# Delta attention of the last layer in chunks of 32 tokens, all batches in lockstep, one quarter of the partitions per head

## The reference, cut to what matters

```python
q, k = l2norm(q), l2norm(k); v = v * beta; kb = k * beta      # beta = sigmoid(x @ Wb), per token and head
# per chunk of 32 tokens: T = inverse of (I + strictly lower part of kb @ k^T)
u, w = T @ v, T @ kb
def step(S, (qi, ki, ui, wi)):                                 # over the chunks, in order
    attn = where(i >= j, qi @ ki^T, 0)
    u_i = ui - wi @ S
    o_i = qi @ S + attn @ u_i
    return S + ki^T @ u_i, o_i
```

## Time and profile before

| | us |
|---|---|
| runs of the kernel before, median of 3 | 8943.74 |
| lowest and highest run | 8923.92, 8946.13 |
| the profiled execution, its own time | 8934.45 |
| its span, first to last instruction | 8932.6 |
| sublayer 6 up to its router, in that span (7437.3 to 8450.4) | 1013.1 |

### The profile page before, as it was taken

One profiled execution on the slowest core, in us unless ns is written; L12 is line 12 of the kernel. 1 busy time (PEld: TensorE's weight loads), 2 busy tenths in 40 slices (PEclk: granted clock), 3 DMA queues, 4 the chain that ended last, 5 costly groups with the idle time before them and its releaser, 6 DMA issues. The chain is left out here.

```text
span 8932.6 us, 296414 instructions
## 1 busy us (share of the span) xinstructions
PE 7426.1 (83%) x129614; PEld 5361.2 (60%) x129614; DVE 5916.2 (66%) x11095; ACT 4144.6 (46%) x6987; POOL 2904.6 (33%) x2116
## 2 busy tenths in 40 slices
PE   7998799999996987987987997997986784756666
PEld 3443588888885665665665665665664453645634
DVE  6664477777776876876866866866866667244266
ACT  3554244444444765765765765765752122111121
POOL 0110122222223753754754745745730000100000
PEclk9998699999998999999999999999998896555556
DMA  0000000000001221221212212212210000000000
GB/s 14 1 1 1 5 5 5 5 5 5 5 3 50 72 59 47 73 54 52 73 50 57 70 47 61 69 44 66 69 40 0 14 0 2 3 2 2 4 0 12
DMA packets 190372, 256.44 MB, mean 29 GB/s; under 512 B 58253, under 2 KB 84748, under 8 KB 188172
## 3 DMA queue, kind: packets, MB, share of 16 engines
q1 hardware_dynamic: 189068, 237.31, 10.0%
HBM read 27.45 MB, written 2.10 MB: 3 GB/s over the span
## 5 line engine op out<-in xcount | busy, mean ns | idle before, releaser
L1758 PE MATMUL wa_front<-w_wqkv,wa_xsT 128*128 128x512 f32 x2400 | 1197.7, 622 | 53.2 <-PEq L66 24.4
L1680 POOL TENSOR_TENSOR XNT<-XNT 128x1024 f32<-128x1024 f32 x396 | 938.2, 2369 | 257.3 <-DVE XNT L1864 257.3
L1683 POOL TENSOR_TENSOR XNT<-XNT,wa_rnorm 128x1024 f32<-128x1024 f32 x396 | 754.2, 1904 | 438.1 <-DVE wa_rnorm L1872 438.1
L1861 DVE TENSOR_TENSOR XNT<-wa_front,w_scaled 128x1024 f32<-128x1024 f32 x396 | 472.4, 1193 | 381.2 <-ACT wa_sq L1699 279.8
L1758 PEld LDWEIGHTS wa_front<-w_wqkv,wa_xsT 128*128 128x128 f32 x2400 | 416.8, 194 | 387.5 <-issue 364.8
L1699 ACT ACTIVATE wa_sq<-wa_front 128x1024 f32<-128x1024 f32 x402 | 408.5, 1016 | 222.6 <-PE wa_front L1758 222.6
L1864 DVE TENSOR_TENSOR XNT<-wa_front,w_scaled 128x512 f32<-128x512 f32 x792 | 505.7, 680 | 0.0
L1877 DVE TENSOR_REDUCE wa_norm<-wa_sq 128x16 f32<-128x1024 f32 x396 | 478.7, 1209 | 0.0
L446 PE MATMUL a0h_ring<-a0h_QT,a0h_KT 32*128 32x512 f32 (+3 forms) x1536 | 449.0, 556 | 14.3 <-ACT a0h_E L564 10.4
L564 ACT ACTIVATE a0h_E<-a0h_ring 128x512 f32<-128x512 f32 (+1 forms) x640 | 320.6, 554 | 287.9 <-PE a0h_ring L446 285.8
L1764 PEld LDWEIGHTS wa_front<-consts,XNT 128*128 128x128 f32 x3168 | 358.7, 142 | 150.6 <-issue 74.5
(11 more groups left out here) (582 smaller groups left out, 18296.2 us busy)
## 6 DMA issues: line engine op xcount, KB each, us to landing
wa_v_look<-wa_v_all SPq DMA_DIRECT2D x1188, 128.0 KB, 2.3
wa_v_look<-wa_v_all SPq DMA_DIRECT2D x792, 64.0 KB, 2.0
w_wqkv<-in_L_ffn_Wqkv_dram SPq DMA_DIRECT2D x6, 1024.0 KB
w_wo<-in_L_ffn_Wo_dram SPq DMA_DIRECT2D x6, 512.0 KB
w_wqkv<-in_L_ffn_Wqkv_dram SPq DMA_DIRECT2D x12, 256.0 KB
f2w_raw<-in_L_ffn_w_dram SPq DMA_DIRECT2D x48, 64.0 KB, 1.9
out_dram<-X SPq DMA_DIRECT2D x1, 2048.0 KB, 8.7
w_w<-in_L_ffn_W_dram SPq DMA_DIRECT2D x6, 341.0 KB
```

Of the source, the lines that this page charges most:

```text
L1680: g.tensor_tensor(rot[:, at], rot[:, at], part[:, at], ALU.add).then_inc(s[summed], 1)
L1683: g.tensor_tensor(rot[:, at], rot[:, at], spread(rnorm[:, at, :], HDW), ALU.mult).then_inc(s[done], 1)
L1758: last = pe.matmul(front[:, first + i, :], xsT[:, slot, :], wqkv[:, (2 * n + i) * 512:(2 * n + i + 1) * 512], start=True, stop=True)
L1861: v.tensor_tensor(rot[:, n], src, cos, ALU.mult)
```

## The change

The chunks become 32 tokens long, as in the reference, and the batches are no longer worked in pairs: there are four paths stages and then a single chunk stage, in which a step covers 4 chunks x 4 batches = 16 matrices for each head. Head h lives on partitions quarter(h), in SBUF and in the array, through all products. Levels 5 and 6 are gone, and with them Nc, T64, Zt6. Keys are not normalized: their norm goes into the factor bp = beta/(k.k) of the rows, and v is multiplied by the norm. The product with w is made once a step (WT), and the recurrence runs over the 4 chunks of a step one after the other (`look`, `weigh`, `learn`, `remember`), between the levels of the inverse. In the paths stage the keys and v are turned head by head, in 32x32 blocks (`turn_heads`, 128 matmuls each), and the small sums come as 8 + 128 + 128 matmuls in place of 24; the mid convolution goes to `act[:, 2, :]`. The products still go through the same three engines, and no DMA changes.

The diff, cut to its core (declarations, copies of constants and index arithmetic left out):

```diff
+CHUNK3 = 32
+CHUNKS3 = SEQ // CHUNK3
+PER = P // CHUNK3
...
 # l3_paths_steps, PE
+            def turn_heads(out, src, sem):
+                for n in range(CHUNKS3):
+                    at = slice(n * CHUNK3, (n + 1) * CHUNK3)
+                    for h in range(HEADS3):
+                        last = pe.matmul(out[quarter(h), at], src[quarter(h), at], c.ident[quarter(h), quarter(h)], start=True,
+                                         stop=True)
+                last.then_inc(sem, 1)
...
-            turn(rawp[:, 0], qk[:, 1, k], s["tok_ps"])
+            turn_heads(rawp[:, 0], qk[:, 1, b], s["ktok_ps"])
             pe.wait_ge(s["sq_ready"], 2)
+            sm = rawp[:, 2]
             for t in range(BLOCKS):
...
+                pe.matmul(sm[:, t * HEADS3:(t + 1) * HEADS3], act[:, 0, t * P:(t + 1) * P], c.head_blocks[:, 0:P:HD3],
+                          start=True, stop=True)
+            for n in range(CHUNKS3):
+                at = slice(n * CHUNK3, (n + 1) * CHUNK3)
+                for h in range(HEADS3):
+                    pe.matmul(sm[quarter(h), CHUNKS3 + n:CHUNKS3 + n + 1], act[quarter(h), 1, at], c.ones[quarter(h), 0:1],
                               start=True, stop=True)
+            for n in range(CHUNKS3):
+                at = slice(b * SEQ + n * CHUNK3, b * SEQ + (n + 1) * CHUNK3)
+                for h in range(HEADS3):
+                    last = pe.matmul(sm[quarter(h), 2 * CHUNKS3 + n:2 * CHUNKS3 + n + 1], XNT[:, at], wb[:, h:h + 1],
+                                     start=True, stop=True)
             last.then_inc(s["small_ps"], 1)
             pe.wait_ge(s["silu_ready"], 3)
             turn(rawp[:, 1], vh[:, MID - 1:], s["path_ps"])
+            pe.wait_ge(s["ktok_kept"], 1)
+            turn_heads(rawp[:, 0], vh[:, MID - 1:], s["vtok_ps"])
...
 # l3_paths_steps, DVE, after the 7-tap convolution
+            v.tensor_scalar(rnq[:, b].rearrange("p t h -> p (t h)"), rawp[:, 2, QS], L2_EPS, None, ALU.add)
+            v.tensor_scalar(ss[:], rawp[:, 2, KS], L2_EPS, None, ALU.add).then_inc(s["sums_ready"], 1)
...
+            v.wait_ge(s["vtok_ps"], 1)
+            v.tensor_tensor(outs[:, mine, 2, :].rearrange("p t (n e) -> p t n e", n=PER),
...
+            convolve(act[:, 2, :], vh[:], wide_taps[:, LOCAL:], MID).then_inc(s["path_ready"], 1)
...
 # l3_chunk_steps, PE: tiny = [P, PER * BATCH, 32]
+            def each(ms, out, lhs, rhs, first=None, end=None):
+                for m in ms:
+                    for h in range(H):
+                        p = quarter(h)
+                        last = pe.matmul(out[p, m, :], lhs(p, m), rhs(p, m), start=first in (None, m), stop=end in (None, m))
+                return last
...
+                    each(every, ztp, whole(lev[:, n]), rhs).then_inc(s["zt_ps"], 1)     # zt(n)
...
+                    pe.wait_ge(s["zt_ready"], 4 * q + n)                                # tx(n)
+                    pe.wait_ge(s["X_ready"], LX * q + n)
+                    if n < SMALL - 1:
+                        each(every, tps, whole(XT[:, q % 2]), whole(Zt)).then_inc(s["t_ps"], 1)
+                    each(every, xps, whole(Zt), whole(XT[:, q % 2])).then_inc(s["x_ps"], 1)
...
+                    each(ms, ups, whole(XT[:, r % 2]), values, first=ms[0], end=M)      # look(n)
+                    pe.wait_ge(s["S_ready"], k + 1)
+                    each(ms, ups, whole(WT), lambda p, m: S[p, m % BATCH, :], first=M, end=ms[-1]).then_inc(s["u_ps"], 1)
...
+                    each(ms, ops, lambda p, m: S[p, m % BATCH, :], chan(0, r), first=ms[0], end=M)
...
+                    pe.wait_ge(s["u_ready"], k + 1)                                     # learn(n)
+                    for m in ms:
+                        for h in range(H):
+                            p = quarter(h)
+                            last = pe.matmul(sps[p, m % BATCH, :], k_tok[p, k, m % BATCH, :], u[p, m % BATCH, :], start=(m == ms[0]),
+                                             stop=(m == ms[-1]))
+                    last.then_inc(s["s_ps"], 1)
+                    last = each(ms, ops, lambda p, m: u[p, m % BATCH, :], whole(AT[:, r % 2]), first=M, end=ms[-1])
...
+                if q is not None:                                                       # the order of a step
+                    each(every, gram, chan(1, q), chan(1, q)).then_inc(s["gram_ps"], 1)
+                if r is not None:
+                    pe.wait_ge(s["W_ready"], r + 1)
+                look(0)
...
+                    each(every, qkp, chan(1, q), chan(0, q)).then_inc(s["qk_ps"], 1)
+                zt(0)
+                learn(0)
+                for n in range(1, SMALL):
+                    zt(n)
+                    if n < PER:
+                        look(n)
+                    tx(n)
+                    if n < PER:
+                        learn(n)
...
+                    for b in range(BATCH):
+                        last = pe.transpose(qkp[:, b * BATCH:(b + 1) * BATCH, :].rearrange("p a e -> p (a e)"), oT[:, b, :], c.ident)
+                    last.then_inc(s["turned"], 1)
+                if q is not None:
+                    pe.wait_ge(s["X_ready"], LX * q + LX)
+                    each(every, tps, lambda p, m: k_tok[p, PER * q + m // BATCH, m % BATCH, :], whole(XT[:, q % 2])).then_inc(s["w_ps"], 1)
```

More of the change, by code:

```diff
@@ L2447, in _ @@
             def _(v):
-                v.memset(XT[:], 0.0)
-                v.memset(T64[:], 0.0)
+                for i, mask in enumerate((c.strict, c.upto)):
+                    for h in range(HEADS3):
+                        v.tensor_copy(within[quarter(h), i, 0, :], mask[quarter(h), quarter(h)])
                 v.wait_ge(s["loaded"], 160)
@@ L2454, in l3_paths_stage @@
         st.end_step()
[L2456 to L2468, removed]
@@ L2475, in l3_paths_steps @@
+    with Stage(nc, "a3d") as st:
+        l3_chunk_steps(nc, st, c, small, within, qk, bp, nbp, rnq, k_tok, outs)
+def l3_paths_steps(nc, st, XNT, c, b, proj, wb, taps, wide_taps, raw, act, qk, vh, lm, bp, nbp, rnq, k_tok, outs):
     rawp = st.ps("rawp", (P, 3, SEQ))
     mid = st.ps("mid", (P, SEQ))
[L2477 to L2480, removed]
+    ss = st.sb("ss", [P, CHUNKS3])
+    root = st.sb("root", [P, CHUNKS3])
+    tb = st.sb("tb", [P, CHUNKS3])
+    s = st.sems("raw_ready raw_copied conv_ready th_ready silu_ready sq_ready small_ps tanh_ready sums_ready "
+                "roots_ready ktok_ps ktok_kept vtok_ps vtok_kept path_ps path_kept path_ready chain")
@@ L2583, in _ @@
[L2583 to L2593, removed]
@@ L2595, in _, with l3_chunk_steps @@
+            v.wait_ge(s["silu_ready"], 3)
+            convolve(act[:, 2, :], vh[:], wide_taps[:, LOCAL:], MID).then_inc(s["path_ready"], 1)
             v.wait_ge(s["path_ready"], 2)
-            v.wait_ge(s["kn_tok_ready"], 1)
+            v.wait_ge(s["vtok_kept"], 1)
     st.end_step()
-def l3_chunk_steps(nc, st, c, pair, small, qk, S, XT, T64, beta, nbeta, rnorms, kn_tok, outs):
+def l3_chunk_steps(nc, st, c, small, within, qk, bp, nbp, rnq, k_tok, outs):
     H = HEADS3
[L2602 to L2613, removed]
@@ L2634, in _, with whole, chan @@
         def _(pe):
[L2635 to L2640, removed]
+            def each(ms, out, lhs, rhs, first=None, end=None):
[4 more added lines that the diff above has]
+                return last
+            def whole(x):
+                return lambda p, m: x[p, m, :]
             for step in range(steps):
                 q, r = phases(step)
-                Nm, XTm = mats(N), mats(XT)
-                T6 = mats(T64)
+                every = range(M)
+                def chan(i, t):
+                    return lambda p, m: qk[p, i, m % BATCH, (PER * t + m // BATCH) * 32:(PER * t + m // BATCH + 1) * 32]
                 def zt(n):
```

363 lines of the change are left out of this document (141 added, 222 removed).

## The result

| | before | after |
|---|---|---|
| median of the runs beside each other (4 and 4), us | 8944.93 | 8894.79 |
| lowest and highest | 8923.92, 8946.68 | 8887.17, 8897.51 |
| ratio, with its 95% interval | | 0.995 [0.9935, 0.9964] |
| paths stages, all four | 303.5 | 357.1 |
| chunk stages, all | 709.6 | 596.6 |

What follows compares the result with a forecast made beforehand. PE's instruction fetch, in blocks of 256 at 3.6 us each, was taken as the bound. Chunk stage 584 us against 709.6 and paths stages 65 more gave -61, from 8943.7 to 8883; range 8828 to 8925.

Steps and rivals of the forecast that it cites:

- The bound of the chunk stage: Chunk stage: PE's instruction fetch sets the pace, 161.9 blocks of 256 instructions, 584 us against 709.6.
- The block's price: Chunk stage: each block of 256 PE instructions takes 3.6 us to fetch; 3.4 gives 552 us, 4.02 gives 652.
- All the rest of the chunk step hidden: Chunk stage: PE's own 35 us a step and the work of DVE, ACT and POOL lie behind the fetch.
- the two waits that were left open: Chunk stage: PE waits at zt(1) for T, up to 1 us, and at tx(4), 1.0 us; each fits in 1.85 us.
- the block's slack: Chunk stage: each fetched block leaves PE 3.6 - 1.75 = 1.85 us for waits.
- The paths stages: Paths stages: 528 PE calls before the 25 taps start these 16.4 us later a batch, 65 us over four.
- The Wb calls: Paths stages: 128 calls a batch with 128x32 weights, 46 ns a record, add 4.7 us over two blocks.
- In hand at PE's start: Paths stages: a block and a half already fetched on average, so v's last block is the seventh, landing at 26 us.
- The sum: Whole kernel: 584 + 65 - 709.6 = -61 us, giving 8883.
- 1, the fetch hidden: Rival for chunk and paths stages: "issue" has another cause and does not return, 324 us for 584, total 8601; chance 0.07.
- 2, the block growing to 4.0: Rival: waits lengthen each block from 3.6 to 4.0 us, 64 us more in chunk stage, 11 in paths, 8958; chance 0.18.
- 3, single-column matmuls at the price of a full one: Rival for paths stages: the 128 Wb calls take 55 us instead of 12 a batch, 172 more, 9055; chance 0.08.

Runs made afterwards that it cites:

- b1: The kernel before the change with the calls of zt(1) to zt(4) issued twice, 128 more in each of 16 steps: chunk stages 827.9 us against 709.6.

## Why the prediction was right, and where it was off

**The bound of the chunk stage: right.** 283 us of "issue", 161 packets (161.9 less 1.5 in hand were forecast), no holes, 15 us of waits for other engines where 50 would have refuted it, and each block resumes 1.2 to 1.6 us after its packet has landed. The runs with more and fewer calls follow the count of packets, not the array's time.

**The block's price: too low by 0.1 us.** The step said 3.6 with four spaces of the earlier trace rows behind it. The mean over the whole stage is 591.1 us (7816.38 to 8407.46) in 160 blocks, 3.69; b1's 3.70 says that it was so before the change. 160.4 x 3.69 + 7 is 599, and 596.6 was measured; forecast were 584. The reason given for taking no more, that the spaces shown still held waits, was wrong: waits inside a space hardly lengthen it (3.70 to 3.68). The DMA view's 3.67 was the better number and stood in the text already.

**All the rest of the chunk step hidden: right.** POOL's mask took 1274 ns (1.2 was the estimate):

```profile
L2770 POOL TENSOR_TENSOR a3d_lev<-a3d_N,a3x_small 128x512 f32<-128x512 f32 x40 | 49.6, 1274 | 453.4 <-DVE a3d_N L2810 453.4
```

It made PE wait once. Of the two waits that were left open, the one of tx(4) for ACT's copy is there (0.8 us, 8 times) and the one of zt(1) for T came at most once (0.9; PEld's list puts it down to POOL's mask). Two that the sum had as covered showed too, tx's tps half for the copy of zt (3 times, 0.8) and the product w for DVE's addition (8 times, up to 1.0, 3.3 us in all). All of them fit in the block's slack.

**The paths stages: right in kind, 53.6 for 65.** The timeline of batch 1, the longest of the four, shows the steps of the sum, from the start of turning the keys at 7569.98:

```profile
7569.98 1.67 PEld L2500 LDWEIGHTS a3p_rawp<-consts,a3x_qk 32*32 32x32 f32 x115 [16.03 <-issue]
...
7573.43 1.79 PEld L2500 LDWEIGHTS a3p_rawp<-consts,a3x_qk 32*32 32x32 f32 x128 [1.78 <-issue]
...
7577.26 3.58 PE L2515 MATMUL a3p_rawp<-consts,a3p_act 128*128 128x4 f32 x16
...
7588.64 1.89 PE L2525 MATMUL a3p_rawp<-a3x_wb,XNT 128*32 128x1 f32 x128 [1.40 <-issue]
...
7593.05 0.19 DVE L2596 TENSOR_SCALAR a3x_rnq<-a3p_rawp 128x32 f32<-128x32 f32 x1 [12.07 <-ACT a3p_tb L2556]
...
7599.32 0.61 PEld L2500 LDWEIGHTS a3p_rawp<-consts,a3p_vh 32*32 32x32 f32 x37 [2.44 <-issue]
...
7600.12 1.22 DVE L2605 TENSOR_TENSOR a_outs<-a3p_rawp,a3p_root 128x1024 f32<-128x1024 f32 x1 [4.43 <-PE a3p_rawp L2500]
7601.26 0.74 DVE L2577 TENSOR_SCALAR a3p_act<-a3p_vh,a3x_wide_taps 128x1024 f32<-128x1024 f32 x1
```

The 25 taps start 31.3 us after PE's start, 14.3 later than before; 33.3 and 16.4 were forecast. DVE stands 12.07 + 4.43 = 16.5 us ahead of them (18). In the four batches they start 29.3, 31.3, 30.8 and 29.9 us after PE's start, where it was 16.95 or 16.96 each time before: 12.3, 14.3, 13.8 and 13.0 later, 53.4 in all, which is the 53.6 of the stages.

Three terms were mis-sized and partly cancel. The Wb calls cost nothing beyond their block: 128 records in 1.89 us, under 15 ns each and not 46, at a granted clock of 0.50 (1.2 GHz); that is -4.7. In hand at PE's start were 171, 115, 188 and 132 loads, 1.2 blocks of 128 on average and not one and a half; in batch 1 eight blocks had to land in place of seven. The last of them came 27.0, 29.3, 28.1 and 28.4 us after the start, where 26 was forecast without the Wb term. And of the 29.3 of batch 1 about 1.3 are the eight q sums, 128x128, 3.58 us, in one block with small calls: the second block behind it landed 8.26 us after it (7576.90 to 7585.16), not two times 3.47. With only one block ahead, a slow block holds back the fetch, which is read from this timeline and was not tried. That v's turning, and no longer the small sums, was the last thing DVE waited for, was as forecast; the runs with DVE transposes then gave back 29.5 us, and with the wide sums 43.3.

**The sum.** -113.0 and +53.6 for -126 and +65: both terms came out some 12 us smaller than forecast, with opposite signs, which is why -59 stands so near to -61. The hit is partly luck.

**The rivals.** 1, the fetch hidden (8601), is refuted by the 283 us of "issue" and by the runs with changed counts. That is also the answer to the rule in the Trainium skill, Runtime: NRT & Kernel Launch, section "Instruction fetch mechanics", that fetching is mostly hidden: for float32 products of 32x32 it is not, since 64 calls run in 1.75 us and the next 64 arrive every 3.69. 2, the block growing to 4.0, was nearer than it looked: the mean is 3.69, and 3.8 was its point; but the block did not grow, since the 33 spaces of 3.3 to 4.02 us in pair 0's stage before average 3.69 as well. 3, single-column matmuls at the price of a full one, is refuted by under 15 ns a record.

## What to carry to other kernels

Where PE runs many small float32 matmuls, count its instructions (four to a call), divide by 256, and compare that number times 3.7 us with the stage: if they meet, fewer calls help, and waits of up to a microsecond inside a block cost next to nothing (3.70 us for 3.68 here). A restructuring that removes waits but adds calls gives part of its gain back; here the transposes of 32x32 blocks on an idle DVE (711 ns for 128x512), wide sums in place of single-column ones and one set for two products with the same weights brought 169 us without the last and 185 with it, on top of the change's 52. Take the price of a repeating unit from the mean over a long stretch, not from a handful of spaces on the timeline. And where a run is to show what waits cost, look first whether the waits are in its trace.

## What the runs showed of the hardware that was not expected

- Matmuls with one moving column and weights of 128 rows x 32 columns went in under 15 ns each (128 in 1.89 us), as fast as 32x32 ones (128 in 1.93 us), at a granted clock of 0.50.
- The space between blocks of instructions takes few values: 3.47 or 3.48 most often (35 of 158), 3.75 (32), and values near 3.34, 3.6, 3.9 and 4.02. The tenths are in part the packet's own: in the 49 spaces under 3.5 us it takes 0.98 us and starts 1.11 us after PEld resumed, in the 88 of 3.7 and over 1.19 us and 1.27 us. Why it does is open.
- A float32 transpose of 32x32 blocks by DVE costs 711 ns for 128x512 and 1.20 to 1.25 us for 128x1024. There is no clear difference between PSUM (the first line) and SBUF (the second) as its source:

```profile
L2593 DVE STREAM_TRANSPOSE a3p_raw<-a3p_mid 128x1024 f32<-128x1024 f32 x4 | 5.0, 1244 | 0.0
L2589 DVE STREAM_TRANSPOSE a3p_raw<-a3p_vh 128x1024 f32<-128x1024 f32 x4 | 4.8, 1202 | 0.0
```
